# A fused graph network kernel: edge scores from an accumulating gather, with more row buffers

## The reference, cut to what matters

```python
x1 = x[edges[0]]
x2 = x[edges[1]]
e = jnp.concatenate([x1, x2], axis=1) @ Ww + bw          # 6144 x 1024
e = e.reshape(-1, H, 2 * HD).transpose(1, 0, 2)          # 8 heads of 128
e = jax.nn.leaky_relu(e, 0.01)
w = (e @ Wa + ba)[..., 0]                                # a score per edge and head
mat = jnp.full((H, n, n), -jnp.inf, jnp.float32)
mat = mat.at[:, edges[0], edges[1]].set(w)
mat = jax.nn.softmax(mat, axis=-1)
...
y = jnp.matmul(mat, out).transpose(1, 0, 2)
```

## Time and profile before

| | |
|---|---|
| runs | 890.57, 892.9, 898.55 us (median 892.9) |
| profiled execution | 893.61 us, its span 891.9 us |
| busy | PE 640.9, DVE 540.2, ACT 264.7, POOL 228.3 us |
| edge stage | gathers from 40.94 us, first sum of rows at 73.02 us, last score at 262.47 us |
| mean granted clock of TensorE | 0.825 of full speed |

### The profile page before, as it was taken

The page is one execution under the profiler, slowest core; times in us unless marked ns, Lnnn a source line. Parts: engine busy times, 40 slices in busy tenths (PEclk is TensorE's granted clock), DMA queues, the critical chain, the costliest instruction groups (busy, mean ns, idle before and its releaser), DMA issues.

```text
span 891.9 us, 9443 instructions
## 1 busy us (share of the span) xinstructions
PE 640.9 (72%) x2807; PEld 305.3 (34%) x2807; DVE 540.2 (61%) x1487; ACT 264.7 (30%) x1089; POOL 228.3 (26%) x232
## 2 busy tenths in 40 slices
PE   5952336423318708982779998618999999999997
PEld 2420112201107704441355544313343443344332
DVE  3457998899878995448454234463446854445533
ACT  2104766557541312441113111011222222222222
POOL 5144677777753510000000000010110111011100
PEclk9985557755556958995788999858999999999999
DMA  8598487788749059103000001182999999999991
GB/s 332 218 382 316 139 260 260 245 275 254 249 138 369 32 174 406 56 0 141 1 0 1 0 0 71 67 336 94 409 417 410 410 406 410 415 420 414 417 362 37
DMA packets 46581, 208.27 MB, mean 234 GB/s; under 512 B 7984, under 2 KB 12592, under 8 KB 36928
## 3 DMA queue, kind: packets, MB, share of 16 engines
q1 hardware_dynamic: 27152, 145.70, 41.0%
q0 software_dynamic: 19376, 61.95, 20.6%
HBM read 199.93 MB, written 10.31 MB: 236 GB/s over the span
## 4 chain that ended last, share of the span: by engine, by line
PE 52%; DVE 7%; DMA 2%; ACT 1%; issue 1%; DVEq 0%; POOLq 0%
PE bank L797 14%; PE bank L825 7%; PE bank L817 6%; PE bank L712 4%; PE bank L727 3%; PE bank L533 2%; PE bank L634 2%; PE bank L640 2%; PE bank L786 2%; PE bank L528 2%; DMA R<-tok_tab,slot_tok 2%; PE bank L745 1%; PE bank L742 1%; DVE sm L1090 1%; PE bank L736 1%; PE bank L686 1%
## 5 line engine op out<-in xcount | busy, mean ns | idle before, releaser
L908 ACT ACTIVATE R<-R 128x128 f32<-128x128 f32 x384 | 113.0, 295 | 109.0 <-DVE R L1211 109.0
L577 PE MATMUL bank<-R 128*128 128x384 bf16 x144 | 50.7, 487 | 125.7 <-DVE R L1172 125.7
L797 PE MATMUL bank<-R 128*64 128x512 f32 (+1 forms) x432 | 108.2, 610 | 0.0
L486 POOL DMA_INDIRECT R<-tok_tab,slot_tok x34 | 34.2, 1005 | 280.2 <-DVE slot_f L1567 272.2
L533 PE MATMUL bank<-R,late 128*128 128x512 f32 x168 | 81.1, 644 | 0.7 <-DMA R<-L_Ww 0.7
L1207 DVE TENSOR_TENSOR R<-R 128x1032 f32<-128x1032 f32 x48 | 59.0, 1230 | 26.9 <-DMA R<-tab_src,e_i 14.0
L825 PE MATMUL bank<-R 128*128 128x512 bf16 x306 | 71.9, 380 | 1.0 <-DVE R L1593 1.0
L1579 DVE TENSOR_TENSOR R<-R,bank 128x256 f32<-128x256 f32 x34 | 14.3, 420 | 95.2 <-ACT R L988 95.2
L908 ACT ACTIVATION_READ_ACCUMULATOR R<-R 128x1 f32 x384 | 71.6, 187 | 0.0
L577 PEld LDWEIGHTS bank<-R 128*128 128x128 bf16 x144 | 13.3, 119 | 158.5 <-DVE R L1172 149.3
L446 POOL DMA_INDIRECT score<-late,e_i x48 | 57.5, 1198 | 30.8 <-DVE late L1166 15.7
(11 more groups left out here) (343 smaller groups left out, 1146.4 us busy)
## 6 DMA issues: line engine op xcount, KB each, us to landing
R<-L_w SPq DMA_DIRECT2D x54, 1536.0 KB, 10.6
late<-L_w SPq DMA_DIRECT2D x18, 1536.0 KB, 9.3
R<-L_w SPq DMA_DIRECT2D x2, 3072.0 KB, 15.0
score<-R POOLq DMA_DIRECT2D x9, 512.0 KB, 13.1
R<-score SPq DMA_DIRECT2D x3, 1536.0 KB, 10.2
R<-L_Ww SPq DMA_DIRECT2D x2, 2048.0 KB, 12.9
R<-L_W SPq DMA_DIRECT2D x4, 1024.0 KB, 9.1
tab_src<-R SPq DMA_DIRECT2D x3, 516.0 KB, 2.7
```

Of the source, the lines that this page charges most:

```text
L577: last = pe.matmul(pb[s][:, 0:N], oh[:, e % 2, 0, P * s:P * s + P], oh[:, e % 2, 1, :], start=(e == 0), stop=(e == ET - 1))
L797: last = pe.matmul(pb[4 + i % 2][part, :], xeT[i % 2][:, k, part], w13[e % NWB][:, k, :], start=(k == 0), stop=(k == KD - 1), tile_positio ...
L908: act_.activation(own, own, ACT.Copy, accum_out=w_e3[:, t, h:h + 1]).then_inc(S("heads_summed"), 1)
```

## The change

- The destination gather writes no buffer of its own. It is an accumulating DMA (`compute_op=ALU.add`) that adds the 128 destination rows onto the source rows in `ga[t]` (`add_dst`). It waits until those source rows have landed. The sum on VectorE (L1207) is gone, and so are the buffers `gd`.
- There are 24 row buffers in place of 13: five more in `late`, six in the space of `Ww`. 24 source gathers are issued ahead of the first `add_dst`; the 24 others follow in the loop at two in three tiles. `add_dst` runs five tiles ahead. A buffer of `ga` comes free with `w_ready`.
- ScalarE sums 6 of 8 heads. VectorE sums the other two itself, with two instructions of 128 elements that have accumulators, and waits for its own pipeline ahead of `add_linear`.
- The destination table has its own staging rows `ab_dst`, so VectorE no longer waits for the store of `tab_src` ahead of L1158.
- The load of the source half of `Ww` is issued second, ahead of the indices; POOL's nine fills of the score table wait for it.
- SP's loads of `Wv` and what follows wait until six tiles are scored (`w_ready` of 6).
- A few semaphores are merged (`most_ready`, `rest_coded`, `xg_cleared`); the four memsets of `xg` are issued one after another with a wait each.

```diff
-NGF = 13
+NGF = 24
+NSRC0 = 18
+AHEAD = 5
+NLS = 4
+HACT = 6
 NGD = 6
...
-        ga = [r1(10240 + ROW * j, ROW) for j in range(7)] + [R2[:, 12288 + ROW * j:12288 + ROW * j + ROW] for j in range(6)]
-        gd = [r1(ROW * j, ROW) for j in range(NGD)]
+        ab_dst = [R2[:, 5656 + ROW * j:5656 + ROW * j + ROW] for j in range(NT)]
+        ga = ([r1(10240 + ROW * j, ROW) for j in range(7)] + [R2[:, 12288 + ROW * j:12288 + ROW * j + ROW] for j in range(6)]
+              + [late[0][:, ROW * j:ROW * j + ROW] for j in range(3)] + [late[1][:, ROW * j:ROW * j + ROW] for j in range(2)]
+              + [r1(ROW * j, ROW) for j in range(6)])
...
             sp.dma_start(x3, xin.rearrange(tiles, p=P)).then_inc(S("x_loaded"), 16)
+            ww = a["L0_Ww"].rearrange("(c p) n -> p c n", p=P)
+            sp.dma_start(Ww[:, 0:4, :], ww[:, 0:4, :]).then_inc(S("Ww_loaded_src"), 16)
...
-            sp.dma_start(Ww[:, 0:4, :], ww[:, 0:4, :]).then_inc(S("Ww_loaded_src"), 16)
...
-                sp.dma_start(tab_dst[P * t:P * t + P, :], ab[t]).then_inc(S("dst_rows_stored"), 16)
+                sp.dma_start(tab_dst[P * t:P * t + P, :], ab_dst[t]).then_inc(S("dst_rows_stored"), 16)
+            sp.wait_ge(S("w_ready"), 6)
...
-            pool.memset(ga[NGF - 1], NEG).then_inc(S("no_token_ready"), 1)
+            pool.memset(ga[NSRC0 - 1], NEG).then_inc(S("no_token_ready"), 1)
             pool.wait_ge(S("no_token_ready"), 5)
+            pool.wait_ge(S("Ww_loaded_src"), 16)
...
             def gather_src(t):
                 j = t % NGF
-                if t == NGF - 1:
+                if t == NSRC0 - 1:
                     pool.wait_ge(S("score_filled"), 16 * 9)
+                if t == NSRC0 + 3:
+                    pool.wait_ge(S("dst_rows_psum"), 2 * NT)
                 if t >= NGF:
-                    pool.wait_ge(S("rows_added"), t - NGD + 1)
+                    pool.wait_ge(S("w_ready"), t - NGF + 1)
+                if t >= NSRC0 + NLS:
+                    pool.wait_ge(S(f"src_rows{t % NLS}"), 16 * ((t - NSRC0) // NLS))
...
+            def add_dst(t):
+                if t == 0:
+                    pool.wait_ge(S("first_src_rows"), 16 * NSRC0)
+                if t >= NSRC0:
+                    pool.wait_ge(S(f"src_rows{t % NLS}"), 16 * ((t - NSRC0) // NLS + 1))
                 if t >= NGD:
-                    pool.wait_ge(S("rows_added"), t - NGD + 1)
-                pool.indirect_dma_start(out=gd[j], out_offset=None, in_=tab_dst[:, :],
-                                        in_offset=bass.IndirectOffsetOnAxis(ap=dst_i[:, t:t + 1], axis=0)).then_inc(S(f"edge_rows{j}"), 16)
+                    pool.wait_ge(S("w_ready"), t - NGD + 1)
+                pool.indirect_dma_start(out=ga[t % NGF], out_offset=None, in_=tab_dst[:, :],
+                                        in_offset=bass.IndirectOffsetOnAxis(ap=dst_i[:, t:t + 1], axis=0),
+                                        compute_op=ALU.add).then_inc(S(f"edge_rows{t % NGD}"), 16)
...
-            for t in range(4):
-                gather_dst(t)
+            for t in range(AHEAD):
+                add_dst(t)
+            later = NGF
             for t in range(ET):
                 if t >= 1:
                     scatter_score(t - 1)
-                if t + 4 < ET:
-                    gather_dst(t + 4)
-                if NGF <= t + 4 < ET:
-                    gather_src(t + 4)
+                if t + AHEAD < ET:
+                    add_dst(t + AHEAD)
+                while later < ET and 1 + (later - NGF) * 3 // 2 <= t:
+                    gather_src(later)
+                    later += 1
...
-                for h in range(H):
+                for h in range(HACT):
                     own = prod[t % 2][:, P * h:P * h + P]
...
-                dve.wait_ge(S("src_rows_stored"), 16 * NT)
...
             def add_linear(t):
-                dve.wait_ge(S("heads_summed"), H * (t + 1))
+                dve.wait_ge(S("heads_summed"), HACT * (t + 1))
+                settle()
...
-                tt(ga[j], ga[j], gd[t % NGD], ALU.add).then_inc(S("rows_added"), 1)
-                dve.wait_ge(S("rows_added"), t + 1)
+                dve.wait_ge(S(f"edge_rows{t % NGD}"), 16 * (t // NGD + 1))
                 if t >= 2:
-                    dve.wait_ge(S("heads_summed"), H * (t - 1))
-                stt(prod[t % 2].rearrange(heads, h=H), ga[j][:, 0:2 * D].rearrange(heads, h=H), 0.0, bc(waR[:, None, :], [P, H, P]),
-                    ALU.max, ALU.mult).then_inc(S("prod_ready"), 1)
+                    dve.wait_ge(S("heads_summed"), HACT * (t - 1))
+                own, terms = ga[t % NGF], prod[t % 2]
+                stt(terms[:, 0:P * HACT].rearrange(heads, h=HACT), own[:, 0:P * HACT].rearrange(heads, h=HACT), 0.0,
+                    bc(waR[:, None, :], [P, HACT, P]), ALU.max, ALU.mult).then_inc(S("prod_ready"), 1)
+                for h in range(HACT, H):
+                    go(stt(terms[:, P * h:P * h + P], own[:, P * h:P * h + P], 0.0, waR, ALU.max, ALU.mult, accum_out=w_e3[:, t, h:h + 1]))
```

More of the change, by code:

```diff
@@ L138, in build @@
         dup_s = R2[:, 1024:1536].bitcast(bf16)
-        prod = [R2[:, 1536:2560], r1(ROW * NGD, 1024)]
+        prod = [R2[:, 1536:2560], r1(ROW * 6, 1024)]
         lsc = prod[0]
         ab = [R2[:, 2560 + ROW * j:2560 + ROW * j + ROW] for j in range(NT)]
-        ga = [r1(10240 + ROW * j, ROW) for j in range(7)] + [R2[:, 12288 + ROW * j:12288 + ROW * j + ROW] for j in range(6)]
-        gd = [r1(ROW * j, ROW) for j in range(NGD)]
+        ab_dst = [R2[:, 5656 + ROW * j:5656 + ROW * j + ROW] for j in range(NT)]
+        ga = ([r1(10240 + ROW * j, ROW) for j in range(7)] + [R2[:, 12288 + ROW * j:12288 + ROW * j + ROW] for j in range(6)]
+              + [late[0][:, ROW * j:ROW * j + ROW] for j in range(3)] + [late[1][:, ROW * j:ROW * j + ROW] for j in range(2)]
+              + [r1(ROW * j, ROW) for j in range(6)])
         mt = [r1(3072 * j, 3072).rearrange("p (n h) -> p n h", h=H) for j in range(NT)]
@@ L262, in rest @@
         def rest(eng, one_expert, before=None, after=None):
-            eng.wait_ge(S("most_ready"), 1)
+            eng.wait_ge(S("over_ready"), 2)
             fullest = eng.value_load(most[0:1, 0:1], min_val=0, max_val=N)
@@ L415, in _ @@
             pool.iota(rec4[:, :, :, 1], pattern=[[P * K3, NT], [1, K3]], base=0, channel_multiplier=K3).then_inc(S("consts_ready"), 1)
-            pool.memset(ga[NGF - 1], NEG).then_inc(S("no_token_ready"), 1)
+            pool.memset(ga[NSRC0 - 1], NEG).then_inc(S("no_token_ready"), 1)
             pool.wait_ge(S("no_token_ready"), 5)
+            pool.wait_ge(S("Ww_loaded_src"), 16)
             fill = score.rearrange("n h -> (n h)").rearrange("(q p c) -> q p c", p=P, c=1024)
             for q in range(9):
-                pool.dma_start(fill[q], ga[NGF - 1][:, 0:1024]).then_inc(S("score_filled"), 16)
+                pool.dma_start(fill[q], ga[NSRC0 - 1][:, 0:1024]).then_inc(S("score_filled"), 16)
             pool.wait_ge(S("edge_idx_ready"), 1)
@@ L427, in gather_src @@
                 j = t % NGF
[L428 removed]
+                if t == NSRC0 - 1:
                     pool.wait_ge(S("score_filled"), 16 * 9)
+                if t == NSRC0 + 3:
+                    pool.wait_ge(S("dst_rows_psum"), 2 * NT)
                 if t >= NGF:
[L431 removed]
+                    pool.wait_ge(S("w_ready"), t - NGF + 1)
+                if t >= NSRC0 + NLS:
+                    pool.wait_ge(S(f"src_rows{t % NLS}"), 16 * ((t - NSRC0) // NLS))
                 pool.indirect_dma_start(out=ga[j], out_offset=None, in_=tab_src[:, :],
[L433 to L436 removed]
+                                        in_offset=bass.IndirectOffsetOnAxis(ap=src_i[:, t:t + 1], axis=0)).then_inc(S("first_src_rows") if t < NSRC0 else S(f"src_rows{t % NLS}"), 16)
+            def add_dst(t):
[3 more added lines that the diff above has]
+                    pool.wait_ge(S(f"src_rows{t % NLS}"), 16 * ((t - NSRC0) // NLS + 1))
                 if t >= NGD:
[L438 to L440 removed]
+                    pool.wait_ge(S("w_ready"), t - NGD + 1)
+                pool.indirect_dma_start(out=ga[t % NGF], out_offset=None, in_=tab_dst[:, :],
+                                        in_offset=bass.IndirectOffsetOnAxis(ap=dst_i[:, t:t + 1], axis=0),
+                                        compute_op=ALU.add).then_inc(S(f"edge_rows{t % NGD}"), 16)
             def scatter_score(t):
@@ L476, in _ @@
             for j in range(NXG):
-                pool.memset(xg[j], 0.0).then_inc(S("xg_cleared"), 1)
+                step(pool.memset(xg[j], 0.0))
             pool.wait_ge(S("tokens_stored"), 16 * (NT + 1))
-            pool.wait_ge(S("xg_cleared"), NXG)
             def gather_tokens(i):
@@ L1157, in _ @@
                     dve.wait_ge(S("dst_rows_psum"), 2 * t + half + 1)
-                    tt(ab[t][:, D * half:D * half + D], pb[(5, 0)[half]][:, :], bwr[:, D * half:D * half + D], ALU.add).then_inc(S("dst_half_ready"), 1)
```

(21 more changed lines are left out.)

1 line of the change is left out of this document (removed).

## The result

| | before | after |
|---|---|---|
| median of four runs | 892.07 us | 908.95 us |
| all runs | 890.57 to 898.55 | 903.67 to 912.19 |
| profiled execution, its span | 893.61, 891.9 | 912.19, 910.4 |
| first product of a tile | 74.3 | 82.13 |
| last score sum | 262.47 | 277.30 |

The ratio of the runs is 1.0173, with a 95% interval of 1.0113 to 1.0234: the changed kernel is slower, by 1.1 to 2.3%. The forecast was 877 us, faster, with a range from 861 to 908.

The account below looks back on a forecast made before the run. POOL's indirect DMAs were taken to bound the edge-stage loop. The last score sum was to move from 262.5 to 245.5 us, 17 us off the profiled 893.6, giving 876.6, predicted as 877 us; range 861 to 908.

Parts of the forecast that it names:

- The bound: Edge-stage loop: POOL sets the pace with three indirect DMAs a tile at 1.38 us each, VectorE close behind.
- The front: Before the loop: gather 22 waits for 18, first add near 73.5 us, landing at 78.7; loop starts 4.4 us later.
- POOL in the loop: POOL's 108 instructions after the first scatter: 149.4 us at 1.38 each, plus 6 us for the adds' issue.
- I take the scatter's: POOL's issue of an add priced like a scatter's, 0.14 us over the destination gather, 6 us for 42.
- DMA in the loop: DMA engines' time for an accumulating gather, bounds 1.26 and 3.2 us; the engines are not the bound.
- under 2.2: The time in us taken for one accumulating gather on the DMA engines in the loop.
- the first rival: DMA engines become the bound: 889 us at 2.52 us an add; chance 0.23 (adds 2.2 to 2.8), 0.25 above.
- The second rival: POOL's issues return to 1.24 us without VectorE's row sum beside them, 15 us more gone: 862 us; chance 0.10.
- 13 fewer gathers in the loop: Count of source gathers said to leave POOL's loop, leaving 24; also used against the first rival.
- VectorE: VectorE's work in the loop: 2.67 us a tile, 128 us for 48, hidden by POOL.
- The moved heads: The two heads' sums moved from ScalarE to VectorE in the loop: gain nothing in time.
- After the loop: Read-back and all later blocks: shift as a whole with the last score sum, microsecond for microsecond.

Follow-up runs that it names:

- runs 1 to 3: run 1; the changed kernel with adds of half the bytes, 903.3 us; run 1 with two small memsets on POOL ahead of each loop destination gather, 906.4 us.
- run 1: The changed kernel with plain destination gathers that overwrite the row buffer in place of adding, the sum of the rows left out: 882.5 us, ratio 0.9845.
- run 7: The changed kernel with 13 source buffers in place of 24, the other 35 source gathers one a tile, adds kept: 913.9 us, ratio 1.0182.
- run 6: All 8 heads summed on ScalarE: the changed kernel so altered 918.1 us, ratio 1.0263; the same with plain gathers 882.8 us, 0.9861.
- run 5: The kernel before with the change's front parts and 18 source buffers in place of 13, plain gathers: 890.1 us, ratio 0.9952.
- run 8: The changed kernel with plain destination gathers, row sum back on VectorE, 18 source buffers, later source gathers spread, 8 heads on ScalarE: 885.1 us, ratio 0.9913.

## Why the prediction was wrong

The profiled execution came to 912.2 where the sum gave 876.6. By its own steps:

- *The bound* was read rightly. POOL sets the pace of the loop; runs 1 to 3 and 7 show it.
- *The front*: right in kind, 3.4 us short. The first add went out at 75.26 (forecast 73.5), and gather 22 waited 6.16 us for the landing of gather 18, as foreseen. The other half is the landing itself: 6.9 us from that issue to the first product, where 5.2 was taken. It isn't the add, nor the 24 gathers: a plain one took 6.2 in run 1 (76.14 to 82.31), an add behind 13 gathers 6.5 in run 7 (65.20 to 71.68). The rows before had 7.2 for this very first gather (65.81 to 73.02); 5.2 is the median of all 48.
- *POOL in the loop* is where it failed. The step "I take the scatter's" put the accumulating issue at 0.14 us over the plain one; it measured 0.65 over (1.70 against 1.05). For 42 adds that is 27 us where the sum had 6, so the term is 21 us short; by the runs the dear issue costs 20 to 22 us in all. The upper bound, 1.68, was right to within 0.02, but that is luck: its row is a scatter whose issue was stretched beside VectorE's row sum (last section), and the shortest scatter is 0.98. The middle was taken from scatters and gathers because these are alike in the rows. An accumulate isn't like them: its shortest issue is 1.53, theirs 0.94 to 0.98.
- The rest of that step: first product to last sum was forecast at 245.5 - 78.7 = 166.8 us. Run 1, which lacks the dear issue, took 166.7. That it fits to 0.1 us is luck, since the forecast had 6 us for the add's issue in it. From the first scatter (86.61) to the last destination gather (241.06) run 1's 108 issues are 1.44 us apart, not 1.38, which is 6.4 us more. POOL's waits for scatters to land, 5.9 us in that run, are of that size. In the changed kernel the same 108 issues are 1.68 us apart (87.27 to 267.31), 26.1 us over the forecast.
- *DMA in the loop*: "under 2.2" failed as well. The add is 1.26 + 1.26 = 2.5 us of full engines, an estimate from the queue's time and the value of the first rival. By itself it costs about 7 us in the profiled loops.
- *The first rival* had the right mechanism in the DMA engines and the wrong size: 889 us. It took POOL's time as covered. The sum lacked the case in which one act makes both resources dearer at once. The chance of 0.25 for a slower kernel stood on adds of over 2.8 us of full engines; slower came true, but not by that way.
- *The second rival*, faster issues without the row sum, didn't come: what stretches them, 14.7 us in the loop before, is 14.4 us in the changed kernel, now beside the product (last section).
- "13 fewer gathers in the loop" is a miscount: there were 48 - 13 = 35 and are 48 - 24 = 24, so 11 fewer. The sum uses the 24 and isn't touched.
- *VectorE* was right: 2.67 us of work a tile was forecast, it is busy 126.9 / 48 = 2.64, and idle for over a third of the loop. *The moved heads* are worth a few us in the profiles, not nothing. *After the loop* I had assumed a pure shift; it was 3.8 us longer, most of it far behind the read-back.

The parts add up: 3.4 for the start, 28.4 for the loop and 3.8 behind it are the 35.6 us between 876.6 and 912.2.

## What to carry to other kernels

Moving an add from a compute engine into a DMA moves it onto two resources, the engine that issues and the DMA engines; ask how full both are before asking what VectorE saves. Here VectorE, which wasn't the bound for most of the loop, lost 1.26 us of work a tile, and POOL, the bound, got 0.65 more. Where an operation has no row in the trace, keep the range as wide as its upper bound on every resource that it touches, added up. Where two engines take turns as the bound, more buffers alone gave nothing (run 5); with the gathers spread as well (run 8) the last score came 5 us sooner (253.62 against 258.57), though the timed runs don't tell the two apart.

## What the runs showed of the hardware

- An accumulating indirect DMA of 128 rows holds POOL for 1.70 us in the mean and 1.53 at the shortest; a plain gather for 1.05 to 1.08 in the mean (runs before and 1) and 0.94 at the shortest. With rows half as long the accumulating one is still 1.66.
- On the DMA engines it costs about twice a gather of the same bytes: 244 us of queue time against 184 for the same 61.95 MB, and 194 with adds of half the bytes.
- POOL's DMA issues stretch now and then by up to 1.1 us, with adds and without. The rows show beside what: an issue that starts while one of VectorE's long instructions runs ends only a fixed time after that instruction. First before, with the gather of the earlier trace rows that ends at 112.31, 0.82 us after the row sum; then after, with the one of 1.35 us shown above, that ends at 191.73, 0.85 us after the product:

```profile
110.27 1.22 DVE L1207 TENSOR_TENSOR R<-R 128x1032 f32<-128x1032 f32 x1
```

```profile
189.92 0.96 DVE L1224 SCALAR_TENSOR_TENSOR R<-R,sm 128x768 f32<-128x768 f32 x1 [0.77 <-DMA R<-tab_dst,e_i]
```

From 80 to 284 us, 26 issues before and 25 after are over 0.2 us longer than the shortest of their kind. All 26 start during the row sum and all 25 during the product. Plain ones and scatters end 0.82 to 0.91 us after it, adds 1.40 to 1.48. So VectorE slows POOL, the bound, at points where POOL waits for nothing of it. The wider product of run 6 stretches more, as it should by this, but no run changes this alone, and the mechanism behind it is not shown.
